# Sparse experts: five full chunks and one shared tail chunk, results turned back by transposes

## What is computed

```
h1 = jnp.einsum('nc,ehc->neh', flat, w1)      # 64 channels to 682 hidden
h3 = jnp.einsum('nc,ehc->neh', flat, w3)
h = jax.nn.silu(h1) * h3
y = jnp.einsum('neh,ech->nec', h, w2)          # 682 hidden to 64 channels
out = jnp.einsum('ne,nec->nc', gates, y)       # gates are 0 but for two experts
```

## Time and profile before

| | us |
|---|---|
| median of 3 runs | 3234.24 (3233.38 to 3239.25) |
| profiled execution, its own time | 3251.35 |
| its span | 3249.5 |
| TensorE matmul busy in the span | 1954.1 (60%) |
| TensorE weight load busy | 1260.2 (39%) |
| VectorE busy | 1554.2 (48%) |
| ScalarE busy | 1170.1 (36%) |
| GpSimd busy | 832.8 (26%) |

### The profile page before, as it was taken

The page is one execution under the profiler, slowest core; times in us unless marked ns, Lnnn a source line. Parts: engine busy times, 40 slices in busy tenths (PEclk is TensorE's granted clock), DMA queues, the critical chain, the costliest instruction groups (busy, mean ns, idle before and its releaser), DMA issues. The chain is left out here.

```text
span 3249.5 us, 34030 instructions
## 1 busy us (share of the span) xinstructions
PE 1954.1 (60%) x9965; PEld 1260.2 (39%) x9965; DVE 1554.2 (48%) x2768; ACT 1170.1 (36%) x1971; POOL 832.8 (26%) x1010
## 2 busy tenths in 40 slices
PE   2699947886999730510004009999925420399995
PEld 1555524555555420500003005555525310255553
DVE  7633355336333467387877004444472640144443
ACT  4466623223566542424121004444412200144442
POOL 0311100002111100000014763444423447344442
PEclk7599978985999855555555559999957655699998
DMA  1000000000000000000013104444346221244443
GB/s 39 10 0 0 0 5 1 0 0 20 1 0 0 2 0 0 1 0 0 0 36 78 34 30 136 132 131 131 104 106 119 79 48 32 73 132 132 131 131 132
DMA packets 201035, 163.12 MB, mean 50 GB/s; under 512 B 157260, under 2 KB 172364, under 8 KB 200652
## 3 DMA queue, kind: packets, MB, share of 16 engines
q1 hardware_dynamic: 182732, 140.89, 15.2%
q0 software_dynamic: 18176, 20.75, 2.0%
HBM read 77.26 MB, written 29.82 MB: 33 GB/s over the span
## 5 line engine op out<-in xcount | busy, mean ns | idle before, releaser
L1067 PE MATMUL ffn_up_ps<-ffn_turned,ffn_up_now 128*114 128x512 f32 x1872 | 516.1, 412 | 6.3 <-remote 2.6
L1160 DVE TENSOR_TENSOR ffn_hidden<-ffn_silu,ffn_up_ps 114x512 f32<-114x512 f32 x468 | 321.3, 686 | 407.5 <-ACT ffn_silu L1127 362.4
L1127 ACT ACTIVATE ffn_silu<-ffn_up_ps 114x512 f32<-114x512 f32 x468 | 281.1, 601 | 445.7 <-PE ffn_up_ps L1067 248.1
L1022 POOL DMA_INDIRECT results<-ffn_yout,ffn_dest x312 | 300.2, 962 | 472.4 <-DVE ffn_yout L1142 399.9
L1067 PEld LDWEIGHTS ffn_up_ps<-ffn_turned,ffn_up_now 128*114 128x114 f32 x1872 | 310.4, 179 | 175.4 <-issue 62.6
L637 ACT ACTIVATE ffn_hidden<-ffn_up_ps,ffn_b 128x512 f32<-128x512 f32 x512 | 310.4, 697 | 0.0
L789 POOL DMA_INDIRECT slots<-ffn_rows,ffn_slot x256 | 245.7, 960 | 139.8 <-issue 77.5
L1053 PE MATMUL ffn_x_ps<-ident,ffn_xin 128*128 128x128 f32 x312 | 48.8, 280 | 362.7 <-DMA ffn_xin<-slots 362.7
L588 PE MATMUL ffn_y_ps<-ffn_hidden,ffn_down 128*64 128x512 f32 x1024 | 247.5, 605 | 0.0
L1149 DVE TENSOR_TENSOR ffn_turned<-ffn_x_ps,ffn_turned 128x512 fp32r<-128x512 f32 x78 | 53.4, 684 | 345.0 <-issue 345.0
L1079 PE MATMUL ffn_y_ps<-ffn_hidden,ffn_down 114*64 114x512 f32 (+1 forms) x936 | 218.2, 601 | 0.0
(11 more groups left out here) (379 smaller groups left out, 3477.2 us busy)
## 6 DMA issues: line engine op xcount, KB each, us to landing
ffn_up_now<-ffn_up SPq DMA_DIRECT2D x78, 682.0 KB
ffn_down<-in_ffn_w SPq DMA_DIRECT2D x78, 192.0 KB, 2.4
ffn_xin<-slots SPq DMA_DIRECT2D x78, 160.0 KB, 2.8
ffn_stage<-in_ffn_w SPq DMA_DIRECT2D x64, 170.5 KB, 3.0
ffn_xin<-slots SPq DMA_DIRECT2D x78, 128.0 KB, 2.6
ffn_both<-results SPq DMA_DIRECT2D x16, 512.0 KB, 6.9
sht_mix<-in_sht_weights SPq DMA_DIRECT2D x8, 1024.0 KB, 8.2
results<-ffn_yout,ffn_dest POOLq DMA_INDIRECT x312
```

Source lines behind the costliest of these rows:

```text
L1022: nc.gpsimd.indirect_dma_start(k.results, bass.IndirectOffsetOnAxis(dest[:, g % AR, q:q + 1], 0), yout[:, g % YR, q, :], None).then_inc(y_ ...
L1067: last = nc.tensor.matmul(up_ps[w][n % 2][0:sizes[c], :], up[:, g % 2, w, c * size:c * size + sizes[c]], turned[:, g % 2, part, :], start= ...
L1127: nc.scalar.activation(silu[0:sizes[c], n % 2, :], up_ps[0][n % 2][0:sizes[c], :], ACT.Silu)\
L1160: nc.vector.tensor_tensor(hidden[0:sizes[c], g % 2, c, :], silu[0:sizes[c], n % 2, :], up_ps[1][n % 2][0:sizes[c], :], ALU.mult).then_inc( ...
```

## The change

The hidden columns are cut into five full chunks of 128 for each of w1 and w3, and the 42 that are left of each share a sixth chunk: w1's tail in its columns 0 to 41, w3's in 64 to 105. For that the host lays both matrices out in one array of 1386 columns an expert, loaded in two pieces of 693. The sixth chunk needs two matmuls in place of four; its silu reads rows 0 to 41 of the bank and writes partitions 64 to 105, its hidden lies there, and its down matmul has 42 rows of contraction from partition 64 (CHUNKS is 5, TAIL 42, UP_PIECE 693). The fold's matmuls become four transposes, and VectorE adds the halves in a second instruction of take_y.

```
-    chunks = -(-HID_B // P)
-    size = -(-HID_B // chunks)
-    sizes = [min(size, HID_B - c * size) for c in range(chunks)]
+    chunks = CHUNKS + 1
+    of_chunk = [slice(0, P)] * CHUNKS + [slice(CH, CH + TAIL)]
...
                     for w in (0, 1):
-                        for part in (0, 1):
-                            last = nc.tensor.matmul(up_ps[w][n % 2][0:sizes[c], :],
-                                                    up[:, g % 2, w, c * size:c * size + sizes[c]],
-                                                    turned[:, g % 2, part, :], start=(part == 0), stop=(part == 1))
-                        last.then_inc(up_done, 1)
+                        first, cols = ((w * CHUNKS + c) * P, P) if c < CHUNKS else (2 * CHUNKS * P, CH + TAIL)
+                        if c < CHUNKS or w == 0:
+                            for part in (0, 1):
+                                last = nc.tensor.matmul(up_ps[w][n % 2][0:cols, :], up[:, g % 2, first:first + cols],
+                                                        turned[:, g % 2, part, :], start=(part == 0), stop=(part == 1))
+                            last.then_inc(up_done, 1 if c < CHUNKS else 2)
...
-                                                down[0:sizes[c], g % 2, c, :],
-                                                hidden[0:sizes[c], g % 2, c, :], start=(c < 2), stop=(c >= chunks - 2))
+                                                down[of_chunk[c], g % 2, c, :],
+                                                hidden[of_chunk[c], g % 2, c, :], start=(c < 2), stop=(c >= chunks - 2))
...
                     for q in range(GROUP):
-                        last = nc.tensor.matmul(out_ps[:, q * CH:(q + 1) * CH], total[:, q * P:(q + 1) * P],
-                                                k.fold[:, :], start=True, stop=True)
+                        last = nc.tensor.transpose(out_ps[:, q * P:(q + 1) * P], total[:, q * P:(q + 1) * P],
+                                                   k.ident[:, :])
...
-                        nc.scalar.activation(silu[0:sizes[c], n % 2, :], up_ps[0][n % 2][0:sizes[c], :], ACT.Silu)\
+                        source = slice(0, P) if c < CHUNKS else slice(0, TAIL)
+                        nc.scalar.activation(silu[of_chunk[c], n % 2, :], up_ps[0][n % 2][source, :], ACT.Silu)\
...
-                    nc.vector.tensor_tensor(yout[:, g % YR, :, :],
-                                            out_ps[:, 0:GROUP * CH].rearrange("p (q c) -> p q c", c=CH),
-                                            gate[:, g % AR, :].unsqueeze(2).to_broadcast([P, GROUP, CH]), ALU.mult)\
+                    nc.vector.tensor_tensor(y_gated[:, :, :], out_ps[:, :].rearrange("p (q c) -> p q c", c=P),
+                                            gate[:, g % AR, :].unsqueeze(2).to_broadcast([P, GROUP, P]), ALU.mult)\
+                        .then_inc(halves_gated, 1)
+                    dve.wait_ge(halves_gated, g + 1)
+                    nc.vector.tensor_tensor(yout[:, g % YR, :, :], y_gated[:, :, 0:CH], y_gated[:, :, CH:P], ALU.add)\
                         .then_inc(y_ready, 1)
...
-                        nc.vector.tensor_tensor(hidden[0:sizes[c], g % 2, c, :], silu[0:sizes[c], n % 2, :],
-                                                up_ps[1][n % 2][0:sizes[c], :], ALU.mult).then_inc(hidden_done, 1)
+                        linear = up_ps[1 if c < CHUNKS else 0][n % 2]
+                        nc.vector.tensor_tensor(hidden[of_chunk[c], g % 2, c, :], silu[of_chunk[c], n % 2, :],
+                                                linear[of_chunk[c], :], ALU.mult).then_inc(hidden_done, 1)
```

More of the change, by code:

```diff
@@ L709 @@
 TOKENS = TILES * P
+CHUNKS = HID_B // P
+TAIL = HID_B - CHUNKS * P
+UP_COLS = 2 * CHUNKS * P + CH + TAIL
+UP_PIECE = UP_COLS // 2
 BLOCK = GROUP * P
@@ L738, in sb @@
             return ctx.enter_context(nc.sbuf_tensor(f"{name}_{n}", shape, dt))
-        up_parts = sb("up", [P, E, 2, HID_B], F32R)
+        up_parts = sb("up", [P, E, 2, UP_PIECE], F32R)
         block_expert, block_place = sb("block_expert", [P, SLOT_BLOCKS], I32), sb("block_place", [P, SLOT_BLOCKS], I32)
@@ L763, in sparse_stage @@
             pad_slot = sbi("pad_slot", [P, E], I32)
-            stage = sbi("stage", [P, 2, HID_B])
+            stage = sbi("stage", [P, 2, UP_PIECE])
             turn_memory(k, sbi, psi, False, E)
@@ L780, in sparse_stage @@
             staged = [sem(f"{name}_staged0"), sem(f"{name}_staged1")]
-            W = [dram[f"{name}_w1"], dram[f"{name}_w3"]]
-            loads = [(w, e) for w in range(2) for e in range(E)]
+            W = dram[f"{name}_up"]
+            loads = [(e, piece) for e in range(E) for piece in (0, 1)]
             N_SMALL = 6
@@ L875, in _ @@
                 sp.dma_start(later[:, :], dram["moe_later"]).then_inc(loaded, 16)
-                for n, (w, e) in enumerate(loads):
+                for n, (e, piece) in enumerate(loads):
                     if n >= 2:
@@ L879, in _ @@
                     for half in (0, 1):
-                        sp.dma_start(stage[half * CH:(half + 1) * CH, n % 2, :], W[w][:, e, :])\
+                        sp.dma_start(stage[half * CH:(half + 1) * CH, n % 2, :], W[:, e, piece, :])\
                             .then_inc(staged[n % 2], 16)
@@ L938, in _ @@
                 pc = Chain(pool, sem(f"{name}_pool"))
-                for n, (w, e) in enumerate(loads):
+                for n, (e, piece) in enumerate(loads):
                     pool.wait_ge(staged[n % 2], 32 * (n // 2 + 1))
-                    pc.link(nc.gpsimd.tensor_copy(up_parts[:, e, w, :], stage[:, n % 2, :]))
-                    low = up_parts[CH:P, e, w, :]
+                    pc.link(nc.gpsimd.tensor_copy(up_parts[:, e, piece, :], stage[:, n % 2, :]))
+                    low = up_parts[CH:P, e, piece, :]
                     nc.gpsimd.tensor_tensor(low, stage[CH:P, n % 2, :], low.bitcast(F32), ALU.subtract)\
@@ L964, in sparse_stage @@
             down = sbi("down", [P, 2, chunks, CH])
-            up = sbi("up_now", [P, 2, 2, HID_B], F32R)
+            up = sbi("up_now", [P, 2, UP_COLS], F32R)
             turned = sbi("turned", [P, 2, 2, BLOCK], F32R)
@@ L969, in sparse_stage @@
             total = sbi("total", [P, BLOCK])
-            yout = sbi("yout", [P, YR, GROUP, CH])
+            yout, y_gated = sbi("yout", [P, YR, GROUP, CH]), sbi("y_gated", [P, GROUP, P])
+            halves_gated = sem(f"{name}_halves_gated")
             x_loaded = [sem(f"{name}_x_loaded{i}") for i in range(XR)]
@@ L1007, in _ @@
                         sp.wait_ge(up_done, 2 * chunks * (g - 1))
-                    sp.dma_start(up[:, g % 2, :, :].rearrange("p w h -> p (w h)").bitcast(F32),
+                    sp.dma_start(up[:, g % 2, :].bitcast(F32),
                                  up_parts[:, expert, :, :].rearrange("p e w h -> p (e w h)").bitcast(F32))\
@@ L2694, in lay_out @@
     for n, src in (("ffn2", "L2_ffn"), ("ffn3", "L3_ffn")):
-        chunks = -(-HID_B // P)
+        cut = CHUNKS * P
         a[f"{n}_router"] = np.asarray(i[f"{src}_router_w"]).T
[L2697 to L2703, removed]
+        w1, w3 = (np.asarray(i[f"{src}_{w}"]).transpose(2, 0, 1) for w in ("w1", "w3"))
+        gap = np.zeros((CH, E, CH - TAIL), np.float32)
+        a[f"{n}_up"] = np.concatenate([w1[..., :cut], w3[..., :cut], w1[..., cut:], gap, w3[..., cut:]], 2)\
+            .reshape(CH, E, 2, UP_PIECE)
+        w2 = np.asarray(i[f"{src}_w2"]).transpose(2, 0, 1)
+        a[f"{n}_w2"] = np.zeros((P, E, CHUNKS + 1, CH), np.float32)
+        a[f"{n}_w2"][:, :, :CHUNKS] = w2[:cut].reshape(CHUNKS, P, E, CH).transpose(1, 2, 0, 3)
+        a[f"{n}_w2"][CH:CH + TAIL, :, CHUNKS] = w2[cut:]
     a["dc_w1"] = np.asarray(i["L1_conv_w1"]).reshape(CH, 16)
```

## The result

| | us |
|---|---|
| before, median of 4 runs | 3233.81 (3230.99 to 3239.25) |
| after, median of 4 runs | 3314.66 (3310.56 to 3316.85) |
| ratio | 1.0242, 95% interval 1.0228 to 1.0257 |
| profiled execution of after, its own time (span) | 3316.85 (3315.1) |

What follows compares the result with a forecast made beforehand. TensorE's pace was taken to bound the 78 sparse expert blocks. Fold with take_y -0.21 and down product +1.00 gave +0.79 us a block, 62 us in all: 3234 to 3296 us, range 3262 to 3330 (0.8).

Steps and rivals of the forecast that it cites:

- The down product: Sparse expert blocks, TensorE: c4 and c5 run one after the other, adding 1.00 us a block (bounds 0 to 1.25).
- an overlapping pair: Rival, down product: c4 and c5 still overlap, product stays 2.73, -16 us in all, 3218 us; chance 0.15.
- changes that cancel: Rival: part of the pair's overlap remains and the sum falls within 0.2%, 3228 to 3241 us; chance 0.04.
- program order: Rival, down product: halves served in program order, product 0.57 longer, net 0.36 a block, 3262 us; chance 0.04.
- The fold with take_y: Blocks: transposes save 0.52 us, longer take_y delays c0's hidden and c2; net -0.21 a block (bounds -0.2 lost, 0.52 gained).
- the tail's move to partitions 64 up has no row: ScalarE and VectorE on c5's chain: the move taken at nothing, at most 0.1 us.
- the 128 columns against 114: Up matmuls of the other five chunks: wider columns cost nothing, at most 0.04 us a block.
- The up product: c5's two matmuls fewer save 0.46 us of work but gain nothing; the wait before c1 grows from 0.18 to 0.64.
- VectorE as a second pacer: Rival, take_y: the add takes 0.94 against GpSimd's traffic; with the serial pair +94 us, 3328 us; chance 0.03.

Runs made afterwards that it cites:

- tail_64: Kernel before, with c5's down matmul taking only rows 0 to 63 of its 112; 3311.95 us, ratio 1.0229 to before.
- pad_tail: Changed kernel, with c5's down matmul over all 128 partitions and its hidden zeroed once before the blocks; 3240.73 us, ratio 1.0013 to before.
- tail_96: Kernel before, with c5's down matmul taking only rows 0 to 95 of its 112; 3235.47 us, ratio 1.0005 to before.
- turn_back_alone: Kernel before, with only the fold's four transposes and the two-instruction take_y of the change; 3224.13 us, ratio 0.9966 to before.
- pad_tail_fold_mm: Changed kernel with c5's 128-row down matmul, old fold and old take_y, leaving only the new up-product cut; 3240.78 us, ratio 1.0022 to before.

## Why the prediction came out as it did

**The down product: right, in place and in size.** Forecast +1.00 (two steps and a boundary, 0.43 + 0.48 + 0.09), measured 0.99. tail_64 shows the loss without the rest of the change, pad_tail shows the rest without the loss. The rivals of an overlapping pair and of changes that cancel fell with the 42-row weights at 2109.26. That of program order, where the product grows by 0.57, fell with 3.71; in tail_96 a 96-row matmul of c5 is in flight beside one of c4 at 2104.35, and two steps of 0.43 and 0.53 follow one another there (weights at 2104.03, c3 at 2104.99) for the four records of c4 and c5. The prediction read such a pair as c4's second matmul standing between two firsts in the code; the code has one call for each chunk, which the profile shows as two records. By records, c5's first starts at 2104.032 in tail_96, before c4's second at 2104.455; by calls, c4 starts first (2104.026) and ends first. So whether this breaks the strict order of matmuls that the Trainium skill states (TensorE: Matmul & The Clock Gate, The mechanism) hangs on which of the two it counts, and no run here decides it.

**The fold with take_y: the term of the sum that was mis-sized.** I put -0.21; by itself it is -0.19, but beside the new cut it is only 10.08 - 10.13 = -0.05, and with the cut's own 0.02 the two come to 10.08 - 10.11 = -0.03. By steps: c3 to c5 2112.59 - 2110.26 = 2.33, forecast 1.93 + 0.35 = 2.28; c5 to c2 3.89, forecast 3.76; c2 to the down product 1.13, forecast 1.10. Together these steps are 0.21 over the forecast (the down product gives 0.02 back, 3.71 for 3.73). Of it 0.12 is a term that I had put at nothing with the bound of 0.1 on c5's chain: "the tail's move to partitions 64 up has no row". What follows that hidden on VectorE starts 0.73 after it instead of 0.60, and take_y, the add and c0's hidden all stand between it and c2. About 0.04 is the 128 columns against 114, the bound that I had left out of the sum: from turn_back_alone to pad_tail the median of c3 to the fold goes from 1.95 to 1.97 and that of c2 to the down product from 1.11 to 1.13. The rest lies in the single blocks that I read; before's c3 to the fold is 1.96 in the median and 1.93 in the block of the earlier trace rows. With this size the sum reads -0.03 + 0.99 = 0.96 a block, x 78 = 75 us, in place of my 62.

**The up product: right in the sum, not quite in the place.** No gain, as forecast; pad_tail_fold_mm has it alone. But I let c0 start 0.46 sooner and put the whole wait before c1. The timeline shows that c0 itself waits for c4's hidden (2113.48, 0.18 for VectorE) after only two matmuls of c5. In the median it starts 0.57 after c5's second, where 0.23 is the pace, so most of the saving, 0.34, became a wait before c0. The wait before c1, forecast to grow by 0.46, grew by 0.05: from c0's last matmul to c1's first it is 0.46, where before had 0.41. c5 to c1 is 2.11, forecast 2.10.

**VectorE as a second pacer** fell: the add takes 0.42, not 0.94.

**What remains.** 75 of 81 us are in the blocks. The other 6 lie within the interval of the ratio, and no stage could be named for them.

## What to carry to other kernels

When matmuls run side by side on halves of the array, look at what each edit does to their shapes: here an operand of 42 or 64 rows beside one of 128 or 114 cost the whole overlap, one of 96 cost nothing, and filling the 42 rows up with zeros gave the overlap back. A saving in front of a wait is worth what can be moved into that wait, so take the waits of the period as a list and reorder against them. Then look at the queues: a load that stands behind another's wait has a due time too, and a step moved forward by a tenth of a period can pass it.

## What was not expected of the hardware

- Two column halves with 114 and 96 rows of contraction are in flight together in tail_96, as two of 114 are; with 114 and 64 they run one after the other. What counts as one shape changes somewhere between 64 and 96 rows.
- A boundary between the shapes of 114 and 64 rows, passed once more in each block by a whole pair, costs 0.14 us.
- VectorE's instruction after one of 42 partitions from 64 on starts 0.72 to 0.73 us after it, in after and pad_tail alike; after one of 112 or 128 partitions from 0 on it is 0.60. All have 512 elements and take 0.69 themselves. Another part of after's trace narrows it down: VectorE's copies of 32 partitions (L1439, from 2480.22 on) take some 0.35 each and start 0.23 apart as long as they stay on partitions 0 to 31, or on 32 to 63, but 0.38 apart where they go over from the first to the second. So neither few partitions nor a start behind partition 0 is enough by itself. That the next instruction starts at other partitions would fit both places; on the hidden it wasn't tried.
